# Recurrent layer: two cell products as one operation on a five-column tile, and the order of two waits turned round

## The chip, the cores and the metric

The kernel runs on one core of one Trainium2 chip. The metric is the device time of a whole execution in microseconds (us); of several runs the median is given. The profile is one execution taken by the hardware profiler. Its engines are PE (TensorE, with PEld for the load of its stationary operand), DVE (VectorE), ACT (ScalarE), POOL (GpSimd) and SP (SyncE). A `q` behind an engine (DVEq) means an instruction that the engine's sequencer carries out itself.

## What is computed

The reference is a network on a graph of 1250 nodes with 512 features: an attention layer over edges, a linear attention, a recurrent layer, a second graph layer, a second linear attention and two expert levels. The change lies in the recurrent layer alone. It takes the 1250 nodes as 1250 steps of one sequence (batch 1, hidden size 512):

```python
def step(carry, x_t):
    h_prev, c_prev = carry
    combined = jnp.concatenate((x_t, h_prev), axis=1)
    f_t = jax.nn.sigmoid(combined @ W_f + b_f)
    i_t = jax.nn.sigmoid(combined @ W_i + b_i)
    c_tilde = jnp.tanh(combined @ W_c + b_c)
    c_t = f_t * c_prev + i_t * c_tilde
    o_t = jax.nn.sigmoid(combined @ W_o + b_o)
    h_t = o_t * jnp.tanh(c_t)
    return ((h_t, c_t), h_t)
```

Each step needs h of the step before, so the steps can't overlap.

## The kernel before

The whole network is one program on one core, stage after stage with barriers between. The recurrent layer is `lstm` (line 1091). The share of x in the gates is worked out for all steps ahead of the loop into `xp`. In the loop only the 512 x 2048 product with h is left. The features stand on 128 partitions in four chunks (KC = 4). The work of a step is cut into two halves q = 0, 1 of two chunks each.

The sigmoid is taken as (1 + tanh(z/2))/2, so one tanh serves all four gates; factors of 2 go into scales. The cell variable holds twice the cell: c = 0.5 * (tanh_f + 1) * c + (tanh_i + 1) * c_tilde, and tanh is taken of 0.5 * c.

A step, engine by engine:

- PE (lines 1202 to 1232) does 128 small matmuls with h as the stationary operand. h is held in two float16 parts, a high and a low one. They are done in eight groups of 16 (`rows(par, q, k)`): three groups need only half 0 of h and start on `s_h[0]`; then PE waits for `s_h[1]` and does five more. The last group for bank 0 is the fifth of the eight and signals `s_gates[0]`; the last for bank 1 is the eighth and signals `s_gates[1]`. Twelve further matmuls into the bank `l_spare` follow, which nothing reads.
- VectorE transposes bank q into columns (`to_columns`, L1272), sums three columns for each gate (`add_up`, L1278), and after ScalarE's tanh of the gates (L1242) makes the input product `gi` (L1287), the forget product `gf` (L1288), and the open gate `go` (L1293). The cell sum is L1299. After ScalarE's tanh of the cell (L1245), `high` multiplies go by it twice (L1306 into float16, L1307 into `full`) and `low` (L1312) subtracts one from the other for the low part, which signals `s_h[q]`.
- ScalarE, after the two tanh of the gates and the two of the cell, lays the next step's input into `turn` (L1235, signal `s_input`) and copies h out (L1249).

The order on VectorE is written by hand in `step`: transpose 0, sum 0, transpose 1, gi 0, gf 0, go 0, sum 1, cell 0, gi 1, gf 1, high 0, cell 1, low 0, go 1, high 1, low 1. Engines go through their instructions in order. The order among engines comes from semaphores alone, each counted up once a step. The loop runs over two steps in each pass (`Fori(0, N, 2)`), with the sets of buffers `par` = 0 and 1.

Two VectorE operations have two waits ahead of them: the transpose of half 0 (`s_input` in `step`, then `s_gates[0]` in `to_columns`) and the first product of `high` (`s_open[q]`, then `s_tcell[q]`).

Of the kernel before, what the change touches and what calls it, by code (L numbers as in the profile page):

```python
# [11 lines left out]
ALU = mybir.AluOpType  # L12
ACT = mybir.ActivationFunctionType
# [3 lines left out]
P = 128  # L17
# [3 lines left out]
KC = C // P  # L21
# [822 lines left out]
def kernel_body(nc, d, out):  # L844

    g = Ctx(nc)
    with ExitStack() as life:
# [158 lines left out]
        linear_attention_0(g, d, x, xn)  # L1006
        g.end_phase()
        lstm(g, d, x, xn)
        g.end_phase()
        layer_1(g, d, x, xn, lo_t, dst_t, tile_node, r_table)  # L1010
# [74 lines left out]
GATES = 4  # L1085
M16 = KC * GATES
Z_BITS = 20
# [3 lines left out]
def lstm(g, d, x, h):  # L1091
# [7 lines left out]
    with ExitStack() as s0:  # L1099
        def sb(name, shape, dt=F32, scope=s0):  # L1100
            return scope.enter_context(nc.sbuf_tensor(name, shape, dt))
# [3 lines left out]
        scale = sb("l_scale", [P, 2])  # L1105
        h_scale = sb("l_h_scale", [P, 2])
        with ExitStack() as s1:
# [11 lines left out]
            with nc.Block() as block:  # L1119
                @block.gpsimd  # L1120
                def _(pool):
                    pool.partition_all_reduce(top[:, 1:2], top[:, 0:1], P, RMAX)
# [49 lines left out]
        hp = sb("l_hp", [P, 2, KC, 2 * SPREAD], F16)  # L1172
        turn = sb("l_turn", [P, 2, 2, GATES, 2 * SPREAD])
        z = sb("l_z", [P, 2, 8])
        th = sb("l_th", [P, 2, 8])
        gi = sb("l_gi", [P, KC])
        gf = sb("l_gf", [P, KC])
        go = sb("l_go", [P, KC])
        c = sb("l_c", [P, KC])
        tc = sb("l_tc", [P, KC])  # L1180
        full = sb("l_full", [P, 2, KC])
        half_h = sb("l_half_h", [P, 2])
# [4 lines left out]
        def pair(name):  # L1187
            return [s0.enter_context(g.semaphore(f"l_{name}{q}")) for q in range(2)]

        s_gates, s_turned, s_sum, s_tanh, s_terms, s_open, s_cell, s_tcell, s_full, s_h = [  # L1190
            pair(n) for n in ("gates", "turned", "sum", "tanh", "terms", "open", "cell", "tcell", "full", "h")]
        s_kept = s0.enter_context(g.semaphore("l_kept"))
        s_input = s0.enter_context(g.semaphore("l_input"))
# [36 lines left out]
        @block.scalar  # L1230
        def _(act):
            act.preload_act_table(ACT.Tanh)

            def lay_input(t, par):
                act.activation(turn[:, par, :, :, 0:34:33].rearrange("p q g v -> p q v g"),  # L1235
                               xp[:, bass.ds(t, 1), :].rearrange("p a (q v g) -> p (a q) v g", q=2, v=2),
                               ACT.Copy).then_inc(s_input, 1)

            def step(t, par):
                for q in range(2):  # L1240
                    act.wait_ge(s_sum[q], t + 1)
                    act.activation(th[:, q, :], z[:, q, :], ACT.Tanh, scale=2.0 ** -Z_BITS).then_inc(s_tanh[q], 1)  # L1242
                for q in range(2):
                    act.wait_ge(s_cell[q], t + 1)
                    act.activation(tc[:, 2 * q:2 * q + 2], c[:, 2 * q:2 * q + 2], ACT.Tanh,  # L1245
                                   scale=0.5).then_inc(s_tcell[q], 1)
                lay_input(t + 1, 1 - par)
                act.wait_ge(s_full[1], t + 1)
                act.activation(h[:, :, bass.ds(t, 1)].rearrange("p j a -> p (j a)"), full[:, par, :],  # L1249
                               ACT.Copy).then_inc(s_kept, 1)  # L1250
            act.wait_ge(s_clean, 1)
            lay_input(0, 0)
            with act.Fori(0, N, 2) as t:
                step(t, 0)
                step(t + 1, 1)

        @block.vector
        def _(dve):
            for par in range(2):
                for q in range(2):  # L1260
                    dve.memset(banks[par][q][:, :], 0.0)
            for u in range(2):
                g.link(dve, dve.tensor_copy(half_h[:, u:u + 1], h_scale[:, 0:1]))
            g.link(dve, dve.memset(c[:, :], 0.0))
            dve.memset(turn[:, :, :, :, :], 0.0).then_inc(s_clean, 1)
            g.link(dve, dve.memset(hp[:, 1, :, :], 0.0))
            dve.memset(hp[:, 0, 0:2, :], 0.0).then_inc(s_h[0], 1)
            dve.memset(hp[:, 0, 2:4, :], 0.0).then_inc(s_h[1], 1)

            def to_columns(t, par, q):  # L1270
                dve.wait_ge(s_gates[q], t + 1)
                dve.transpose(turn[:, par, q, :, 1:33],  # L1272
                              banks[par][q][:, 0:128].rearrange("p (m r) -> p m r", r=32)).then_inc(s_turned[q], 1)

            def add_up(t, par, q):
                dve.wait_ge(s_turned[q], t + 1)
                three = turn[:, par, q, :, :].rearrange("p g (v e) -> p v g e", e=SPREAD)[:, :, :, 0:3]
                dve.tensor_reduce(z[:, q, :].rearrange("p (v g) -> p v g", g=GATES), three, AX.X,  # L1278
                                  ALU.add).then_inc(s_sum[q], 1)

            def gate_of(q):
                return slice(2 * q, 2 * q + 2), th[:, q, :].rearrange("p (j q) -> p j q", q=GATES)

            def cell_terms(t, q):
                two, gate = gate_of(q)
                dve.wait_ge(s_tanh[q], t + 1)
                dve.scalar_tensor_tensor(gi[:, two], gate[:, :, 1], 1.0, gate[:, :, 3], ALU.add, ALU.mult)  # L1287
                dve.scalar_tensor_tensor(gf[:, two], gate[:, :, 0], 1.0, c[:, two], ALU.add,  # L1288
                                         ALU.mult).then_inc(s_terms[q], 1)

            def open_gate(t, q):
                two, gate = gate_of(q)
                dve.scalar_tensor_tensor(go[:, two], gate[:, :, 2], 1.0, half_h[:, :], ALU.add,  # L1293
                                         ALU.mult).then_inc(s_open[q], 1)

            def cell_sum(t, q):
                two, gate = gate_of(q)
                dve.wait_ge(s_terms[q], t + 1)
                dve.scalar_tensor_tensor(c[:, two], gf[:, two], 0.5, gi[:, two], ALU.mult,  # L1299
                                         ALU.add).then_inc(s_cell[q], 1)  # L1300

            def high(t, par, q):
                two, gate = gate_of(q)
                dve.wait_ge(s_open[q], t + 1)
                dve.wait_ge(s_tcell[q], t + 1)
                dve.tensor_tensor(hp[:, 1 - par, two, 30], go[:, two], tc[:, two], ALU.mult)  # L1306
                dve.tensor_tensor(full[:, par, two], go[:, two], tc[:, two], ALU.mult).then_inc(s_full[q], 1)  # L1307

            def low(t, par, q):
                two, gate = gate_of(q)  # L1310
                dve.wait_ge(s_full[q], t + 1)
                dve.tensor_tensor(hp[:, 1 - par, two, 31], full[:, par, two], hp[:, 1 - par, two, 30],  # L1312
                                  ALU.subtract).then_inc(s_h[q], 1)

            def step(t, par):
                dve.wait_ge(s_input, t + 1)
                to_columns(t, par, 0)
                add_up(t, par, 0)
                to_columns(t, par, 1)
                cell_terms(t, 0)  # L1320
                open_gate(t, 0)
                add_up(t, par, 1)
                cell_sum(t, 0)
                cell_terms(t, 1)
                high(t, par, 0)
                cell_sum(t, 1)
                low(t, par, 0)
                open_gate(t, 1)
                high(t, par, 1)
                low(t, par, 1)  # L1330
            with dve.Fori(0, N, 2) as t:
                step(t, 0)
                step(t + 1, 1)
            dve.wait_ge(s_h[1], N + 1)
            dve.wait_ge(s_kept, N)
            dve.scalar_tensor_tensor(x[:, :, 0:N], h[:, :, 0:N], h_scale[:, 1:2], x[:, :, 0:N], ALU.mult, ALU.add)
# [311 lines left out]
```

## Time and profile before

| | before |
|---|---|
| median of 3 runs | 8412.2 us (8410.73 to 8414.29) |
| the profiled execution | 8412.73 us, of which 8411.0 are the span from the first to the last instruction |
| mean granted TensorE clock over the span | 0.876 |
| PE busy | 5425.7 us, 65% of the span |
| DVE busy | 4210.5 us, 50% |
| ACT busy | 1532.4 us, 18% |
| POOL busy | 975.8 us, 12% |
| recurrent loop, transposes of L1272 | 2500, from 2480.9 to 6983.0 us |

The shares are means over stages with quite different limits, so they say little of the recurrent loop. It has to be read by itself: first who waits for whom, then the timeline of a single step, where each line gives the start, the duration and, in brackets, how long the engine sat idle and who ended that. The durations of VectorE and ScalarE operations overlap: the next one can start before the one ahead has reported its end, so it is the distance from start to start that an operation costs.

### The profile page before, as it was taken

What the parts mean: (1) busy time and instruction counts of PE and PEld (TensorE: products, weight loads), DVE (VectorE), ACT (ScalarE), POOL (GpSimd) and SP (SyncE); (2) the same over time, 40 slices, a digit from 0 to 9 for tenths busy, and PEclk for the clock granted to TensorE, in tenths of its full rate; (3) what the DMA queues carried; (4) which work ended last, traced back from release to release, by engine and by line L of the source; (5) the groups of instructions that cost most, each with busy time, mean ns of one, the idle gap of its engine ahead of it and who ended that gap; (6) DMA issues with size and microseconds to landing.
All of it is one profiled execution on the core that took longest, in us unless ns stands there. A gap on an engine that the chain in (4) does not pass through costs nothing. (4 is left out here: it accounts for less than half of the span.)

```text
span 8411.0 us, 418391 instructions
## 1 busy us (share of the span) xinstructions
PE 5425.7 (65%) x180989; PEld 3590.3 (43%) x180989; DVE 4210.5 (50%) x25124; ACT 1532.4 (18%) x7811; POOL 975.8 (12%) x1419
## 2 busy tenths in 40 slices
PE   1060007787787777777777777777777776675989
PEld 0020003343345555555555555555555553233435
DVE  5034446631336666666666666666666664324111
ACT  0000000011002222222222222222222221000111
POOL 1606635500000000000000000000000002510000
PEclk7585557798899999999999999999999997577889
DMA  1025553300000000000000000000000001210000
GB/s 62 16 83 161 161 106 111 108 25 25 20 20 0 0 0 0 0 0 0 0 0 0 0 0 0 0 0 0 0 0 0 0 0 42 66 43 20 0 40 13
DMA packets 117023, 236.72 MB, mean 28 GB/s; under 512 B 65357, under 2 KB 68301, under 8 KB 112986
## 3 DMA queue, kind: packets, MB, share of 16 engines
q0 software_dynamic: 56032, 162.48, 7.0%
q1 hardware_dynamic: 60922, 73.33, 2.8%
q8 instruction: 42, 0.69, 0.0%
q14 instruction: 27, 0.22, 0.0%
HBM read 221.30 MB, written 14.45 MB: 28 GB/s over the span
## 5 line engine op out<-in xcount | busy, mean ns | idle before, releaser
L1203 PE MATMUL l_bank<-l_w,l_hp 128*32 128x128 f16 x160000 | 2464.5, 219 | 1236.9 <-DVE l_hp L1312 1231.7
L1203 PEld LDWEIGHTS l_bank<-l_w,l_hp 128*32 128x32 f16 x160000 | 2246.3, 97 | 1871.2 <-DVE l_hp L1312 1865.6
L1272 DVE STREAM_TRANSPOSE l_turn<-l_bank 128x128 f32<-128x128 f32 x2500 | 791.8, 317 | 1159.7 <-PE l_bank L1203 1116.2
L1224 PE MATMUL l_spare<-l_w 128*2 128x512 f16 x15000 | 1026.0, 379 | 0.0
L1242 ACT ACTIVATE l_th<-l_z 128x8 f32<-128x8 f32 x2500 | 521.2, 208 | 2235.0 <-DVE l_z L1278 2235.0
L1245 ACT ACTIVATE l_tc<-l_c 128x2 f32<-128x2 f32 x2500 | 487.7, 195 | 548.7 <-DVE l_c L1299 548.7
L790 POOL COPY conv_idx<-dst_t 128x1 int32 x176 | 33.9, 193 | 4758.8 <-DVE conv_rows L800 4757.4
L1287 DVE SCALAR_TENSOR_TENSOR l_gi<-l_th 128x2 f32<-128x2 f32 x2500 | 381.8, 153 | 261.3 <-ACT l_th L1242 260.9
L1306 DVE TENSOR_TENSOR l_hp<-l_go,l_tc 128x2 f16<-128x2 f32 x2500 | 420.8, 168 | 179.9
L1278 DVE TENSOR_REDUCE l_z<-l_turn 128x8 f32<-128x24 f32 x2500 | 437.4, 175 | 42.6
L1312 DVE TENSOR_TENSOR l_hp<-l_full,l_hp 128x2 f16<-128x2 f32 x2500 | 422.3, 169 | 43.1
L840 PE MATMUL attend_bank<-attend_rows,attend_onehot 128*128 128x512 f32 x704 | 307.7, 582 | 165.7 <-DVE attend_onehot L813 165.0
L162 PE MATMUL forth_ends_bank<-ident,forth_ends 128*8 128x128 f32 x2 | 0.6, 395 | 601.5 <-PEq L127 601.5
L1293 DVE SCALAR_TENSOR_TENSOR l_go<-l_th,l_half_h 128x2 f32<-128x2 f32 x2500 | 383.5, 153 | 0.0
L1288 DVE SCALAR_TENSOR_TENSOR l_gf<-l_th,l_c 128x2 f32<-128x2 f32 x2500 | 383.3, 153 | 0.0
L1307 DVE TENSOR_TENSOR l_full<-l_go,l_tc 128x2 f32<-128x2 f32 x2500 | 383.1, 153 | 0.0
L1299 DVE SCALAR_TENSOR_TENSOR l_c<-l_gf,l_gi 128x2 f32<-128x2 f32 x2500 | 378.2, 151 | 0.0
L1224 PEld LDWEIGHTS l_spare<-l_w 128*2 128x2 f16 x15000 | 305.1, 84 | 152.1
L1249 ACT ACTIVATE xn<-l_full 128x4 f32 x1250 | 262.1, 210 | 409.4 <-DVE l_full L1307 409.4
L840 PE MATMUL conv_bank<-conv_rows,conv_onehot 128*128 128x257 f32 x352 | 211.5, 703 | 147.6 <-DMA conv_rows<-r_table,conv_idx 89.5
L840 PEld LDWEIGHTS attend_bank<-attend_rows,attend_onehot 128*128 128x128 f32 x704 | 160.4, 264 | 312.9 <-DVE attend_onehot L813 174.2
L632 DVE TENSOR_TENSOR q_rows<-q_rows,k_rows 128x512 f32<-128x512 f32 x176 | 124.0, 704 | 307.5 <-DMA k_rows<-k_table,score_idx 307.5
(393 smaller groups left out, 5366.6 us busy)
## 6 DMA issues: line engine op xcount, KB each, us to landing
keys<-in_src_by_tile SPq DMA_DIRECT2D x7, 1344.0 KB, 6.8
e_w<-in_e_W SPq DMA_DIRECT2D x2, 4096.0 KB
w<-in_g_W SPq DMA_DIRECT2D x2, 2048.0 KB, 10.4
l_wh<-in_l_Wh SPq DMA_DIRECT2D x1, 4096.0 KB
l_wx<-in_l_Wx SPq DMA_DIRECT2D x1, 4096.0 KB, 11.9
e_w<-in_e_W SPq DMA_DIRECT2D x2, 2048.0 KB
q_rows<-q_table,score_idx POOLq DMA_INDIRECT x176, 3.4
k_rows<-k_table,score_idx POOLq DMA_INDIRECT x176, 3.6
```

The source lines that it names most:

```text
L840: mm = pe.matmul(banks[i][:, a:b], onehot[:, i, :], rows[:, i, a:b], start=True, stop=True)
L1203: mm = pe.matmul(banks[par][q][32 * j:32 * j + 32, 0:128], hp[:, par, k, 30 - 30 * v:62 - 30 * v], w16[:, part, k, j, 256 * q + 128 * v:25 ...
L1224: pe.matmul(spare[32 * j:32 * j + 2, 0:512], w16[:, 0, k, j, 0:2], w16[:, 0, k, j, :], start=True, stop=True)
L1242: act.activation(th[:, q, :], z[:, q, :], ACT.Tanh, scale=2.0 ** -Z_BITS).then_inc(s_tanh[q], 1)
L1245: act.activation(tc[:, 2 * q:2 * q + 2], c[:, 2 * q:2 * q + 2], ACT.Tanh, scale=0.5).then_inc(s_tcell[q], 1)
L1272: dve.transpose(turn[:, par, q, :, 1:33], banks[par][q][:, 0:128].rearrange("p (m r) -> p m r", r=32)).then_inc(s_turned[q], 1)
L1278: dve.tensor_reduce(z[:, q, :].rearrange("p (v g) -> p v g", g=GATES), three, AX.X, ALU.add).then_inc(s_sum[q], 1)
L1288: dve.scalar_tensor_tensor(gf[:, two], gate[:, :, 0], 1.0, c[:, two], ALU.add, ALU.mult).then_inc(s_terms[q], 1)
L1293: dve.scalar_tensor_tensor(go[:, two], gate[:, :, 2], 1.0, half_h[:, :], ALU.add, ALU.mult).then_inc(s_open[q], 1)
L1306: dve.tensor_tensor(hp[:, 1 - par, two, 30], go[:, two], tc[:, two], ALU.mult)
L1307: dve.tensor_tensor(full[:, par, two], go[:, two], tc[:, two], ALU.mult).then_inc(s_full[q], 1)
L1312: dve.tensor_tensor(hp[:, 1 - par, two, 31], full[:, par, two], hp[:, 1 - par, two, 30], ALU.subtract).then_inc(s_h[q], 1)
```

## The change

The input product `gi` and the forget product `gf` of a half become one operation with four elements per partition. For that, the cell moves into the tile `th`: it now has five columns for each chunk, column 0 the cell, columns 1 to 4 the tanh of the gates f, i, o and c. The operation takes columns 1 and 2 (f, i), adds 1, and multiplies by columns 0 and 4 (cell, c_tilde). The results go to `terms`, whose two columns the cell sum adds into column 0 of `th`. ScalarE's tanh of the gates writes to columns 1 to 4 and the tanh of the cell reads column 0.

Of the two pairs of waits, the order in the text is turned: `s_gates[0]` now stands ahead of `s_input`, and `s_tcell[q]` ahead of `s_open[q]`. No wait is added or taken out.

```diff
--- before.py
+++ after.py
@@ -1172,11 +1172,9 @@
         hp = sb("l_hp", [P, 2, KC, 2 * SPREAD], F16)
         turn = sb("l_turn", [P, 2, 2, GATES, 2 * SPREAD])
         z = sb("l_z", [P, 2, 8])
-        th = sb("l_th", [P, 2, 8])
-        gi = sb("l_gi", [P, KC])
-        gf = sb("l_gf", [P, KC])
+        th = sb("l_th", [P, KC, GATES + 1])
+        terms = sb("l_terms", [P, KC, 2])
         go = sb("l_go", [P, KC])
-        c = sb("l_c", [P, KC])
         tc = sb("l_tc", [P, KC])
         full = sb("l_full", [P, 2, KC])
         half_h = sb("l_half_h", [P, 2])
@@ -1239,10 +1237,12 @@
             def step(t, par):
                 for q in range(2):
                     act.wait_ge(s_sum[q], t + 1)
-                    act.activation(th[:, q, :], z[:, q, :], ACT.Tanh, scale=2.0 ** -Z_BITS).then_inc(s_tanh[q], 1)
+                    act.activation(th[:, 2 * q:2 * q + 2, 1:],
+                                   z[:, q, :].rearrange("p (j m) -> p j m", m=GATES), ACT.Tanh,
+                                   scale=2.0 ** -Z_BITS).then_inc(s_tanh[q], 1)
                 for q in range(2):
                     act.wait_ge(s_cell[q], t + 1)
-                    act.activation(tc[:, 2 * q:2 * q + 2], c[:, 2 * q:2 * q + 2], ACT.Tanh,
+                    act.activation(tc[:, 2 * q:2 * q + 2], th[:, 2 * q:2 * q + 2, 0], ACT.Tanh,
                                    scale=0.5).then_inc(s_tcell[q], 1)
                 lay_input(t + 1, 1 - par)
                 act.wait_ge(s_full[1], t + 1)
@@ -1261,7 +1261,7 @@
                     dve.memset(banks[par][q][:, :], 0.0)
             for u in range(2):
                 g.link(dve, dve.tensor_copy(half_h[:, u:u + 1], h_scale[:, 0:1]))
-            g.link(dve, dve.memset(c[:, :], 0.0))
+            g.link(dve, dve.memset(th[:, :, :], 0.0))
             dve.memset(turn[:, :, :, :, :], 0.0).then_inc(s_clean, 1)
             g.link(dve, dve.memset(hp[:, 1, :, :], 0.0))
             dve.memset(hp[:, 0, 0:2, :], 0.0).then_inc(s_h[0], 1)
@@ -1269,6 +1269,8 @@
 
             def to_columns(t, par, q):
                 dve.wait_ge(s_gates[q], t + 1)
+                if q == 0:
+                    dve.wait_ge(s_input, t + 1)
                 dve.transpose(turn[:, par, q, :, 1:33],
                               banks[par][q][:, 0:128].rearrange("p (m r) -> p m r", r=32)).then_inc(s_turned[q], 1)
 
@@ -1278,42 +1280,37 @@
                 dve.tensor_reduce(z[:, q, :].rearrange("p (v g) -> p v g", g=GATES), three, AX.X,
                                   ALU.add).then_inc(s_sum[q], 1)
 
-            def gate_of(q):
-                return slice(2 * q, 2 * q + 2), th[:, q, :].rearrange("p (j q) -> p j q", q=GATES)
-
             def cell_terms(t, q):
-                two, gate = gate_of(q)
+                two = slice(2 * q, 2 * q + 2)
                 dve.wait_ge(s_tanh[q], t + 1)
-                dve.scalar_tensor_tensor(gi[:, two], gate[:, :, 1], 1.0, gate[:, :, 3], ALU.add, ALU.mult)
-                dve.scalar_tensor_tensor(gf[:, two], gate[:, :, 0], 1.0, c[:, two], ALU.add,
-                                         ALU.mult).then_inc(s_terms[q], 1)
+                dve.scalar_tensor_tensor(terms[:, two, :], th[:, two, 1:3], 1.0, th[:, two, 0:GATES + 1:GATES],
+                                         ALU.add, ALU.mult).then_inc(s_terms[q], 1)
 
             def open_gate(t, q):
-                two, gate = gate_of(q)
-                dve.scalar_tensor_tensor(go[:, two], gate[:, :, 2], 1.0, half_h[:, :], ALU.add,
+                two = slice(2 * q, 2 * q + 2)
+                dve.scalar_tensor_tensor(go[:, two], th[:, two, 3], 1.0, half_h[:, :], ALU.add,
                                          ALU.mult).then_inc(s_open[q], 1)
 
             def cell_sum(t, q):
-                two, gate = gate_of(q)
+                two = slice(2 * q, 2 * q + 2)
                 dve.wait_ge(s_terms[q], t + 1)
-                dve.scalar_tensor_tensor(c[:, two], gf[:, two], 0.5, gi[:, two], ALU.mult,
+                dve.scalar_tensor_tensor(th[:, two, 0], terms[:, two, 0], 0.5, terms[:, two, 1], ALU.mult,
                                          ALU.add).then_inc(s_cell[q], 1)
 
             def high(t, par, q):
-                two, gate = gate_of(q)
+                two = slice(2 * q, 2 * q + 2)
+                dve.wait_ge(s_tcell[q], t + 1)
                 dve.wait_ge(s_open[q], t + 1)
-                dve.wait_ge(s_tcell[q], t + 1)
                 dve.tensor_tensor(hp[:, 1 - par, two, 30], go[:, two], tc[:, two], ALU.mult)
                 dve.tensor_tensor(full[:, par, two], go[:, two], tc[:, two], ALU.mult).then_inc(s_full[q], 1)
 
             def low(t, par, q):
-                two, gate = gate_of(q)
+                two = slice(2 * q, 2 * q + 2)
                 dve.wait_ge(s_full[q], t + 1)
                 dve.tensor_tensor(hp[:, 1 - par, two, 31], full[:, par, two], hp[:, 1 - par, two, 30],
                                   ALU.subtract).then_inc(s_h[q], 1)
 
             def step(t, par):
-                dve.wait_ge(s_input, t + 1)
                 to_columns(t, par, 0)
                 add_up(t, par, 0)
                 to_columns(t, par, 1)
```

## Rows read from the trace of the kernel before

**Rows 1.** Waits in 2480:6984 us: who waited <- for whom, us in total, times, longest.
```profile
ACT l_th L1242 <- DVE l_z L1278: 2235.0, 2500, 3.5
...
PE l_bank L1203 <- DVE l_hp L1312: 1231.7, 1249, 1.1
```

**Rows 2.** Window 2481:6984: us, busy us of PE, PEld, DVE, ACT, POOL; clock, DMA.
```profile
2481.00:6984.00 4503.00, 3270.91 (x174900) 2484.35 (x174888) 2819.49 (x22492) 1313.65 (x7497) 0.00 (x0) 1.00 0.00 0
```

**Rows 3.** Line 1272 in the whole trace: count, duration ns, first and last start us.
```profile
L1272 DVE STREAM_TRANSPOSE l_turn<-l_bank x2500: 316/316/319, 2480.9 to 6983.0; 128x128 f32<-128x128 f32 x193
```

**Rows 4.** Timeline of one step: start us, us, engine, line, operation, idle before it.
```profile
4004.00 1.97 PE L1203 MATMUL l_bank<-l_w,l_hp 128*32 128x128 f16 x128 [1.04 <-DVE l_hp L1312]
...
4005.42 0.32 DVE L1272 STREAM_TRANSPOSE l_turn<-l_bank 128x128 f32<-128x128 f32 x1 [0.83 <-PE l_bank L1203]
...
4005.77 0.18 DVE L1278 TENSOR_REDUCE l_z<-l_turn 128x8 f32<-128x24 f32 x1
...
4005.98 0.21 ACT L1242 ACTIVATE l_th<-l_z 128x8 f32<-128x8 f32 x1 [1.27 <-DVE l_z L1278]
4006.02 0.32 DVE L1272 STREAM_TRANSPOSE l_turn<-l_bank 128x128 f32<-128x128 f32 x1
4006.26 0.13 DVE L1287 SCALAR_TENSOR_TENSOR l_gi<-l_th 128x2 f32<-128x2 f32 x1
...
4006.38 0.15 DVE L1293 SCALAR_TENSOR_TENSOR l_go<-l_th,l_half_h 128x2 f32<-128x2 f32 x1
4006.45 0.17 DVE L1278 TENSOR_REDUCE l_z<-l_turn 128x8 f32<-128x24 f32 x1
...
4006.65 0.21 ACT L1242 ACTIVATE l_th<-l_z 128x8 f32<-128x8 f32 x1 [0.46 <-DVE l_z L1278]
4006.77 0.19 ACT L1245 ACTIVATE l_tc<-l_c 128x2 f32<-128x2 f32 x1
4006.89 0.16 DVE L1287 SCALAR_TENSOR_TENSOR l_gi<-l_th 128x2 f32<-128x2 f32 x1 [0.21 <-ACT l_th L1242]
4006.97 0.15 DVE L1288 SCALAR_TENSOR_TENSOR l_gf<-l_th,l_c 128x2 f32<-128x2 f32 x1
4007.06 0.17 DVE L1306 TENSOR_TENSOR l_hp<-l_go,l_tc 128x2 f16<-128x2 f32 x1
...
4007.39 0.20 ACT L1245 ACTIVATE l_tc<-l_c 128x2 f32<-128x2 f32 x1 [0.44 <-DVE l_c L1299]
4007.40 0.15 DVE L1293 SCALAR_TENSOR_TENSOR l_go<-l_th,l_half_h 128x2 f32<-128x2 f32 x1
```

**Rows 5.** Timeline of the following step, beginning with PE's start.
```profile
4007.55 1.97 PE L1203 MATMUL l_bank<-l_w,l_hp 128*32 128x128 f16 x128 [0.93 <-DVE l_hp L1312]
4007.70 0.17 DVE L1306 TENSOR_TENSOR l_hp<-l_go,l_tc 128x2 f16<-128x2 f32 x1
...
4007.96 0.17 DVE L1312 TENSOR_TENSOR l_hp<-l_full,l_hp 128x2 f16<-128x2 f32 x1
...
4009.08 0.32 DVE L1272 STREAM_TRANSPOSE l_turn<-l_bank 128x128 f32<-128x128 f32 x1 [0.95 <-PE l_bank L1203]
...
4009.57 0.32 DVE L1272 STREAM_TRANSPOSE l_turn<-l_bank 128x128 f32<-128x128 f32 x1
...
4009.89 0.16 DVE L1287 SCALAR_TENSOR_TENSOR l_gi<-l_th 128x2 f32<-128x2 f32 x1
...
4010.11 0.17 DVE L1278 TENSOR_REDUCE l_z<-l_turn 128x8 f32<-128x24 f32 x1
```

**Rows 6.** Line 1271, windows 4005.35:4005.36 and 4008.90:4008.91 us, VectorE's sequencer (DVEq).
```profile
L1271 DVEq EVENT_SEMAPHORE  x1: 21/21/21, 4005.4 to 4005.4; - x1
...
L1271 DVEq EVENT_SEMAPHORE  x1: 21/21/21, 4008.9 to 4008.9; - x1
```

**Rows 7.** Line 1305, windows 4006.99:4007.00 and 4007.63:4007.64 us, VectorE's sequencer.
```profile
L1305 DVEq EVENT_SEMAPHORE  x1: 21/21/21, 4007.0 to 4007.0; - x1
...
L1305 DVEq EVENT_SEMAPHORE  x1: 21/21/21, 4007.6 to 4007.6; - x1
```

## The prediction

> **What bounds the kernel now.** I read the waits of the recurrent layer first [rows 1]. The longest are ScalarE's for the column sums (L1278) and PE's for the line that finishes h (L1312), 2235 and 1232 us: engines waiting for one another in turn, a closed loop with no engine full. TensorE's granted clock is 1.00 over the whole layer, the 2.4 GHz level [rows 2]. Next the length of a step. The transposes run 2500 times, two a step, from 2480.9 to 6983.0 us [rows 3]; the last is the second of its step, 0.6 after the first, so 1249 periods take 4501.5 us: 3.60 us a step. 1250 such steps are 4505 of the 8412.7 us, and nothing else is touched.
>
> The third view is the timeline of one step [rows 4], from PE's start at 4004.00 to the next at 4007.55: 3.55 us. The mean being 3.604, the other step of the two in a loop pass takes 3.66. This one is the pass's second step, the next its first. I name the work by half q: T is the transpose, R the reduction, th the gate tanh, tc the cell tanh. In the second step T0 starts at 5.42 (all times here are 4000 plus), R0 5.77, th0 5.98, T1 6.02, gi0 6.26, then gf0, go0 6.38, R1 6.45, th1 6.65, tc0 6.77, gi1 6.89, gf1 6.97, h0's first product 7.06, and PE again at 7.55 [rows 5]. The reader is to see which of these are held by a producer and which only by the instruction ahead. T1 comes 2.02 after PE's start, when its last matmul is out. It holds gi0: th0 was done at 6.19 but gi0 starts 0.24 behind T1. gf0, go0 and R1 follow it with some 0.07 from start to start, held by nothing but VectorE's issue. th1 follows R1 by 0.20, tc0 follows th1 by 0.12.
>
> In the first step [rows 5], PE starts at 7.55 and T1 at 9.57, again 2.02 later, but T0 starts at 9.08, 1.53 after PE instead of 1.42. It drags th0 and gi0 (9.89, 2.34 after PE, not 2.26), and R1 is at 10.11, 2.56 after PE, not 2.45. That is the whole difference between 3.66 and 3.55.
>
> The last rows say why [rows 6, 7]. An instruction with two waits stands in the program as two: an EVENT_SEMAPHORE of VectorE's sequencer and then the operation. The semaphore instruction carries line 1271 or 1305, the wait written last (s_gates, s_tcell), so the wait written first stays with the operation. At present the late signal is the one in the semaphore instruction. It passed at 5.35, and T0 started 0.07 later; at 8.90, just behind the loop's branch, and T0 started 0.18 later; at 6.99 and 7.06 for h0's product; at 7.63 and 7.70 for h1's. An operation that carries its only wait starts sooner: tanh of half 1 ends at 6.65 + 0.21 = 6.86 and gi1 starts 0.03 later, while tc0 ends at 6.77 + 0.19 = 6.96 and h0's product starts 0.10 later.
>
> **The change, part by part.** *One product fewer for each half.* In half 0, the merged operation takes gi0's place at 6.26, go0 takes gf0's place and R1 takes go0's, 6.38 instead of 6.45: 0.07 earlier. R1 has a floor: it reads T1's output, and R0 followed T0 by 0.35, so R1 can't start before 6.02 + 0.35 = 6.37. The floor is just met. In half 1 the removed gf1 is worth nothing by itself: h0's product was held by tc0 through 6.99, not by gf1. But it must be out of the way: th1 moves to 6.58, the merged operation to 6.82, and with the 0.08 from gi1 to gf1 the issue would allow 6.90.
>
> *The price of the merged operation* isn't in the trace. It has four elements with steps of 5 and 4 words, against two elements. Below: 0, an operation that costs what gi0 costs; less than gi0, with twice the elements, it has no reason to cost. Above: the TENSOR_REDUCE with 24 scattered elements takes 0.18 and the products 0.15 [rows 4], 0.02 to 0.03 more. I take 0.002, two more elements at the 1 ns each that this gap makes, as the operation is nearest to the products. The Trainium skill (Vector Engine (DVE) Microarchitecture Reference, section 5.2) speaks against a tile with five columns: an operand that hops by a few words on every element costs up to 2.5 ns a column instead of 1.05. By it, four elements would add some 6 ns, at most 12 in a step or 15 us in all, and the sum would come out at up to 8184 instead of 8171; no row here has such a step in a product of this size.
>
> *The wait for s_tcell first.* It now stays with h's product and s_open becomes the semaphore instruction. In half 0 go0 is long done, so the instruction passes at once and the product sits ready. tc0, 0.12 behind th1, starts at 6.70, ends at 6.89, and the product starts 0.03 later, 6.92. That is later than the 6.90 of issue, so tc0 sets it. Against 7.06 the two edits together give 0.14. PE follows this product by 0.49 as before: 7.41. In half 1 s_open comes from go1, which VectorE issues just ahead: 7.40 now, 7.26 then, done at 7.41, through the semaphore instruction at about 7.45, and the product 0.07 later, 7.52. So here s_open is the later of the two (tc1 would allow 7.39 + 0.20 - 0.14 + 0.03 = 7.48), and what is queued behind this wait is the two products and low h of half 1. That is 0.11 after PE's start instead of 0.15. Low h of half 1 comes 0.26 later (7.96 after 7.70 now), so it starts 0.37 after PE and ends at 0.54. PE needs it only after 48 of 128 matmuls, about 0.7 by 1.97 for all: covered, by more than now. If the cover were gone, each 0.01 there would cost 12.5 us.
>
> *The wait for s_gates first, s_input moved behind it.* T0 in the second step starts at 5.35 rather than 5.42: hidden, as T1 holds gi0's place at 6.26 (th0's result would be there at 6.15). In the first step T0 starts at 8.90 rather than 9.08, so th0's result no longer holds the products, T1 does, and the first step becomes like the second: 0.11 off. s_input comes from the copy that ScalarE issues right behind tc1 (7.39), over 1 us before T0, so the waiting instruction ahead holds nobody up. Nothing else is moved past any queue, no DMA is in this loop.
>
> *At nothing:* the tanh writing into the tile's columns 1 to 4, tc reading column 0, the sum writing there, and one memset. ScalarE took 0.21 for eight elements and 0.19 to 0.20 for two [rows 4], so shape hardly counts; each 0.01 on th1 or tc0 costs 12.5 us.
>
> **The sum.** Second step 3.55 - 0.14 = 3.41. First step 3.66 - 0.14 - 0.11 = 3.41. Mean 0.195 less, times 1250 is 244 us; the merged operation gives 2 back. From the profiled execution's 8412.7 us this leaves 8171. That execution lies 0.5 us over the median of the runs, which is nothing here.
>
> **The rivals.**
> *A, the loop's start keeps its delay.* The 0.18 behind the branch may be late arrival of the transpose itself, which no order of waits cures. For: the same pair of instructions costs 0.07 elsewhere. Against: the last operation ahead of the branch starts at 7.96 and T0 at 9.08, time enough to bring the transpose in once nothing stands blocked between. Both steps then win 0.14: 8412.7 - 175 = 8238.
> *B, the order of the waits gives nothing*, because the split into two instructions doesn't follow the text, or because both signals pay the same. Then only R1's 0.07 is left: 8412.7 - 88 = 8325. Against it stand [rows 6, 7], where the last-written wait is the separate one. The Trainium skill's rule for chained operations (VectorE: DVE Perf Modes, Rules for kernel authors), minimize the count and not the semaphores, would give this result; the 0.03 against 0.10 speaks against it.
> *C, the five-column tile is dear.* The merged operation costs 0.025 more, before R1 in full, before h0's product less 0.02 of room: 0.03, and 0.01 on the strided tanh. 0.04 a step, 50 us: about 8219.
> *D, slower.* The merged operation holds VectorE as T1 does, 0.24 to the next and not 0.08, because both inputs hop inside one tile. It stands twice in the loop: 2 x 0.16 - 0.02 = 0.30 lost against 0.195 won, 0.105 x 1250 = 131 us more: 8544. It decides from 0.11 extra on (2 x 0.11 - 0.02 = 0.20). Against: T moves 128 elements, this four, and 24 elements cost only 0.03.
>
> **Chances.** Forecast 0.66, A 0.12, C 0.10, B 0.07, D 0.03, and 0.02 for a mixture near no change. The forecast's own range comes from 0.01 of doubt in each of the terms 0.07, 0.07 and half of 0.11, about 20 us each way, so 8150 at the bottom. Upwards C and A are needed to leave out no more than 2 in 10: 8240. A change of 0.2% is about what a measurement of this kernel can tell from none. Only D lies on the slower side: faster 0.95, same 0.02, slower 0.03.
>
> **What would show it.** Both steps alike at 3.41. R1 2.38 after PE. T0 1.35 after PE in both steps. The semaphore instructions long before T0 and h0's product, and 0.03 from tc0's end to the product. The merged operation at 0.15 to 0.17. If the steps still differ by 0.11, A holds; if h0's product still comes 0.10 after tc0, B; if go0 is over 0.08 behind the merged operation, C or D. It would be wrong in another way if PE stood still after 48 matmuls, waiting for half 1.

## The result, and the profile after

The changed kernel takes 8171.7 us (median of 4 runs, 8171.0 to 8175.2) against 8411.5 us (8408.0 to 8414.3) for the kernel before: a ratio of 0.972, 95% interval 0.970 to 0.973, or 240 us less. The profiled execution took 8172.0 us, its span 8170.3.

The page of the changed kernel, its groups of instructions (busy us, mean ns of one; then the idle time ahead of them and who ended it):

```profile
L1201 PE MATMUL l_bank<-l_w,l_hp 128*32 128x128 f16 x160000 | 2464.2, 219 | 998.6 <-DVE l_hp L1310 993.4
...
L1286 DVE SCALAR_TENSOR_TENSOR l_terms<-l_th 128x4 f32<-128x4 f32 x2500 | 357.0, 143 | 256.9 <-ACT l_th L1240 256.9
L1280 DVE TENSOR_REDUCE l_z<-l_turn 128x8 f32<-128x24 f32 x2500 | 446.9, 179 | 42.6
```

PE still does its 160000 matmuls at 219 ns, but it now waits 993 us for VectorE ahead of them, where [rows 1] had 1232. VectorE has one operation fewer for each half: the merged product stands 2500 times, at a mean of 143 ns; each of the two products that it replaces took 153 ns in the mean.

A step in the timeline, from PE's start to the next (columns as in [rows 4]). It is the second of a loop pass; the last two rows belong to the first step of the next pass:

```profile
4003.35 1.97 PE L1201 MATMUL l_bank<-l_w,l_hp 128*32 128x128 f16 x128 [0.80 <-DVE l_hp L1310]
4003.47 0.17 DVE L1304 TENSOR_TENSOR l_hp<-l_go,l_tc 128x2 f16<-128x2 f32 x1
...
4003.73 0.17 DVE L1310 TENSOR_TENSOR l_hp<-l_full,l_hp 128x2 f16<-128x2 f32 x1
...
4004.71 0.32 DVE L1274 STREAM_TRANSPOSE l_turn<-l_bank 128x128 f32<-128x128 f32 x1 [0.80 <-PE l_bank L1201]
...
4005.27 0.21 ACT L1240 ACTIVATE l_th<-l_z 128x8 f32<-128x8 f32 x1 [1.24 <-DVE l_z L1280]
4005.38 0.32 DVE L1274 STREAM_TRANSPOSE l_turn<-l_bank 128x128 f32<-128x128 f32 x1
4005.62 0.12 DVE L1286 SCALAR_TENSOR_TENSOR l_terms<-l_th 128x4 f32<-128x4 f32 x1
4005.66 0.15 DVE L1291 SCALAR_TENSOR_TENSOR l_go<-l_th,l_half_h 128x2 f32<-128x2 f32 x1
4005.73 0.18 DVE L1280 TENSOR_REDUCE l_z<-l_turn 128x8 f32<-128x24 f32 x1
...
4005.94 0.21 ACT L1240 ACTIVATE l_th<-l_z 128x8 f32<-128x8 f32 x1 [0.46 <-DVE l_z L1280]
4006.05 0.19 ACT L1245 ACTIVATE l_tc<-l_th 128x2 f32<-128x2 f32 x1
4006.18 0.16 DVE L1286 SCALAR_TENSOR_TENSOR l_terms<-l_th 128x4 f32<-128x4 f32 x1 [0.21 <-ACT l_th L1240]
4006.28 0.17 DVE L1304 TENSOR_TENSOR l_hp<-l_go,l_tc 128x2 f16<-128x2 f32 x1
...
4006.54 0.17 DVE L1310 TENSOR_TENSOR l_hp<-l_full,l_hp 128x2 f16<-128x2 f32 x1
4006.61 0.20 ACT L1245 ACTIVATE l_tc<-l_th 128x2 f32<-128x2 f32 x1 [0.37 <-DVE l_th L1297]
4006.62 0.15 DVE L1291 SCALAR_TENSOR_TENSOR l_go<-l_th,l_half_h 128x2 f32<-128x2 f32 x1
...
4006.76 1.91 PE L1201 MATMUL l_bank<-l_w,l_hp 128*32 128x128 f16 x124 [0.79 <-DVE l_hp L1310]
...
4008.12 0.32 DVE L1274 STREAM_TRANSPOSE l_turn<-l_bank 128x128 f32<-128x128 f32 x1 [0.80 <-PE l_bank L1201]
```

From PE's start at 4003.35 to the next at 4006.76 the step takes 3.41 us. The reader can lay it beside [rows 4]. T0 comes 1.36 after PE (1.42 before), T1 2.03 (2.02 before). The merged product stands 0.24 behind T1, as gi0 did. The sum of half 1 (R1) follows at 2.38 after PE, not 2.45, tanh of the cell at 2.70, not 2.77, and h's product at 2.93, not 3.06. The next step's T0 stands at 4008.12, again 1.36 after PE's start at 4006.76, where [rows 5] had 1.53: the first step of a pass is no longer the slow one.

The semaphore instruction that now waits for `s_input` (line 1273, VectorE's sequencer, windows 4003.83:4003.84 and 4007.60:4007.61):

```profile
L1273 DVEq EVENT_SEMAPHORE  x1: 21/21/21, 4003.8 to 4003.8; - x1
...
L1273 DVEq EVENT_SEMAPHORE  x1: 21/21/21, 4007.6 to 4007.6; - x1
```

It passes 0.9 and 0.5 us ahead of its transpose (4004.71, 4008.12); the second of the two is the one behind the loop's branch. In [rows 6] it passed 0.07 and 0.18 ahead of it and set its start.

### The profile page after: what moved, and what is told of

The parts are those of the page before. It is cut to its first block and busy times, and to the rows that moved or that the text cites. A ratio compares the mean times of both kernels' runs of the same rounds, so it can differ in the third digit from the quotient of the medians.

```text
span 8170.3 us, 415891 instructions
## 1 busy us (share of the span) xinstructions
PE 5428.9 (66%) x180989; PEld 3593.0 (44%) x180989; DVE 4004.0 (49%) x22624; ACT 1536.1 (19%) x7811; POOL 975.0 (12%) x1419
## 5 line engine op out<-in xcount | busy, mean ns | idle before, releaser
L1245 ACT ACTIVATE l_tc<-l_th 128x2 f32<-128x2 f32 x2500 | 490.8, 196 | 463.8 <-DVE l_th L1297 463.8
L1286 DVE SCALAR_TENSOR_TENSOR l_terms<-l_th 128x4 f32<-128x4 f32 x2500 | 357.0, 143 | 256.9 <-ACT l_th L1240 256.9
L1297 DVE SCALAR_TENSOR_TENSOR l_th<-l_terms 128x2 f32<-128x2 f32 x2500 | 386.0, 154 | 0.0
L1233 ACT ACTIVATE l_turn<-l_xp 128x16 f32 (+1 forms) x1251 | 275.5, 220 | 2.6 <-DVE l_turn L1265 2.6
```

The source lines that it names most:

```text
L1245: act.activation(tc[:, 2 * q:2 * q + 2], th[:, 2 * q:2 * q + 2, 0], ACT.Tanh, scale=0.5).then_inc(s_tcell[q], 1)
L1297: dve.scalar_tensor_tensor(th[:, two, 0], terms[:, two, 0], 0.5, terms[:, two, 1], ALU.mult, ALU.add).then_inc(s_cell[q], 1)
```

## The experiments

Each stands beside runs of the kernel before from the same session. The interval is some 14 us each way, so a few us between two medians mean nothing; where a smaller difference matters, the step from the trace decides. The step is worked out from the first and last transposes of half 0, as the prediction does from [rows 3].

| kernel | median us | before us | ratio (95%) | step us |
|---|---|---|---|---|
| the change | 8171.7 | 8411.5 | 0.972 (0.970 to 0.973) | 3.41 |
| merge_only | 8327.2 | 8408.7 | 0.990 (0.989 to 0.992) | 3.54 |
| waits_only | 8304.9 | 8408.7 | 0.988 (0.986 to 0.989) | 3.52 |
| old_input_order | 8237.8 | 8408.7 | 0.980 (0.978 to 0.981) | 3.47 |
| old_cell_order | 8258.4 | 8408.7 | 0.982 (0.980 to 0.984) | 3.48 |
| five_columns_two_ops | 8305.2 | 8411.8 | 0.987 (0.986 to 0.989) | 3.52 |
| go0_behind_cell0 | 8171.2 | 8411.8 | 0.971 (0.970 to 0.973) | 3.41 |
| half1_old_order | 8172.2 | 8411.8 | 0.972 (0.970 to 0.973) | 3.41 |
| late_half1 | 8176.7 | 8411.8 | 0.972 (0.971 to 0.974) | 3.41 |
| late_half1_384b | 8276.0 | 8408.7 | 0.984 (0.983 to 0.986) | 3.50 |
| low_by_chunks | 8231.7 | 8401.9 | 0.980 (0.978 to 0.982) | 3.47 |

### One part alone: merge_only and waits_only

merge_only is the changed kernel with both pairs of waits in the old order:

```diff
-                dve.wait_ge(s_gates[q], t + 1)
                 if q == 0:
                     dve.wait_ge(s_input, t + 1)
+                dve.wait_ge(s_gates[q], t + 1)
...
-                dve.wait_ge(s_tcell[q], t + 1)
                 dve.wait_ge(s_open[q], t + 1)
+                dve.wait_ge(s_tcell[q], t + 1)
```

> The changed kernel with both pairs of waits in the old order, so the merged product and the five-column tile alone. Theory (the two edits help each other: the merged product brings the sum of half 1 forward by 0.07, the rest of its worth comes only once the late wait stays with the operation): 0.07 a step, 88 us, about 8325; both steps keep their difference of 0.11. Rival (the parts are independent and the merged product brings most of the gain, since it stands twice in the loop): two operations of 0.07, 0.14 a step, about 8237.

waits_only is the kernel before with both pairs turned round and nothing else.

> The kernel before with both pairs of waits turned round, nothing merged. Theory: h's product of half 0 may start as soon as tc0 is out (6.99 in the old timeline) but stands behind the forget product (6.97) by 0.08, so it comes at 7.05 and not at 7.06: 0.01 a step; the first step of a pass loses its extra 0.11; together 0.065 a step, 81 us, about 8331, and the two steps become equal at 3.54. This and the merged product alone then add up to 169 us of the 240 measured. Rival (independent parts): 0.07 + 0.055 a step, 156 us, about 8256.

The merged product alone is worth 82 us, the waits alone 104, together 185 before rounding; the change has both and brings 240. Some 55 us belong to neither part alone. The steps say the same without the noise of the runs: 3.604 before, 3.542 with the merged product, 3.521 with the waits, 3.413 with both, so 0.045 a step (57 us) over the sum of the two parts. The two timelines show where, at the same place of a step. In merge_only (sum of half 1, tanh of the cell of half 0, merged product of half 1, h's product):

```profile
4004.43 0.17 DVE L1280 TENSOR_REDUCE l_z<-l_turn 128x8 f32<-128x24 f32 x1
...
4004.76 0.19 ACT L1245 ACTIVATE l_tc<-l_th 128x2 f32<-128x2 f32 x1
4004.89 0.16 DVE L1286 SCALAR_TENSOR_TENSOR l_terms<-l_th 128x4 f32<-128x4 f32 x1 [0.21 <-ACT l_th L1240]
4005.05 0.17 DVE L1304 TENSOR_TENSOR l_hp<-l_go,l_tc 128x2 f16<-128x2 f32 x1
```

tc0 ends at 4004.76 + 0.19 = 4004.95, and h's product comes at 4005.05, still 0.10 later. It is held by the semaphore instruction, so the room that VectorE now has ahead of it is of no use. In waits_only (tanh of the cell, gi, gf, h's product):

```profile
4004.78 0.19 ACT L1245 ACTIVATE l_tc<-l_c 128x2 f32<-128x2 f32 x1
4004.91 0.16 DVE L1289 SCALAR_TENSOR_TENSOR l_gi<-l_th 128x2 f32<-128x2 f32 x1 [0.21 <-ACT l_th L1242]
4004.99 0.15 DVE L1290 SCALAR_TENSOR_TENSOR l_gf<-l_th,l_c 128x2 f32<-128x2 f32 x1
4005.06 0.17 DVE L1308 TENSOR_TENSOR l_hp<-l_go,l_tc 128x2 f16<-128x2 f32 x1
```

tc0 ends at 4004.97 and its signal would let the product go at 5.00; but gf of half 1 starts at 4.99 and the product stands 0.07 behind it. Here VectorE's issue sets it. Only with both parts, as in the changed kernel, does the product come 0.04 behind tc0 (6.05 + 0.19, product at 6.28). So the order alone moves this product from 0.10 to 0.09 behind tc0, and beside the merged product from 0.10 to 0.04: some 0.05 a step that neither part has alone, which is about the 0.045 left over.

The expectation for waits_only, 8331, was 26 us too high. It took 0.01 a step for half 0's product. The second step fell from 3.55 to 3.52 instead: gf, which did not have to wait for a signal, is followed by the product after 0.07 and not 0.08, and the product, which is no longer held up either, is followed by `full` after 0.07 too.

### The order of the waits, place by place: old_input_order, old_cell_order, half1_old_order

Each is the changed kernel with one of the pairs turned back; half1_old_order turns `s_open` and `s_tcell` back for half 1 alone, and this is its edit:

```diff
+                first, second = (s_tcell, s_open) if q == 0 else (s_open, s_tcell)
-                dve.wait_ge(s_tcell[q], t + 1)
-                dve.wait_ge(s_open[q], t + 1)
+                dve.wait_ge(first[q], t + 1)
+                dve.wait_ge(second[q], t + 1)
```

> The changed kernel with the waits of the transpose of half 0 back in the old order (s_gates in the separate semaphore instruction). Theory (the start of the loop pass is slow only because the transpose can't be brought in while the semaphore instruction blocks): the first step gets its delay back, T0 0.18 behind the semaphore instruction, 0.11 to 0.12 on every other step, 69 to 72 us: about 8242; the second step stays at 3.41. Rival (the order here is hidden in both steps, since T1 holds the products anyway): 8172.

It cost 66 us against the change. Two steps of its timeline:

```profile
4001.06 1.97 PE L1201 MATMUL l_bank<-l_w,l_hp 128*32 128x128 f16 x128 [0.80 <-DVE l_hp L1310]
...
4002.59 0.32 DVE L1274 STREAM_TRANSPOSE l_turn<-l_bank 128x128 f32<-128x128 f32 x1 [0.98 <-PE l_bank L1201]
...
4003.08 0.32 DVE L1274 STREAM_TRANSPOSE l_turn<-l_bank 128x128 f32<-128x128 f32 x1
...
4003.40 0.17 DVE L1286 SCALAR_TENSOR_TENSOR l_terms<-l_th 128x4 f32<-128x4 f32 x1
...
4004.58 1.97 PE L1201 MATMUL l_bank<-l_w,l_hp 128*32 128x128 f16 x128 [0.91 <-DVE l_hp L1310]
...
4006.01 0.32 DVE L1274 STREAM_TRANSPOSE l_turn<-l_bank 128x128 f32<-128x128 f32 x1 [0.88 <-PE l_bank L1201]
```

The step from 4001.06 is the first of a pass: T0 comes 1.53 after PE, the merged product waits for half 0's tanh until 3.40 instead of following T1 (3.08) by 0.24, and the step takes 3.52. The next T0 comes 1.43 after PE, later than the changed kernel's 1.36, and costs next to nothing, as T1 covers it: with a mean of 3.47 and a first step of 3.52, the second takes 3.42 where the change takes 3.41. So the order at this place is worth 0.11 in the first step and at most 0.01 in the second, as the prediction has it. What VectorE's sequencer does in the 0.18 between the semaphore instruction and T0 no view shows: the branch itself is over long before, as the instructions of the loop's end (L1331) stand at 4008.0 to 4008.3 in the kernel before and the semaphore instruction at 4008.90. Shown is only that the delay goes when the late wait stands with the transpose.

> The changed kernel with s_open ahead of s_tcell again in the text, so the late s_tcell is in the separate semaphore instruction. Theory: h's product starts 0.10 after tc0's end, not 0.03, and nothing else covers it: 0.066 in both steps, 83 us, about 8254, both steps 3.48. Rival (half 0's product has other cover and the order costs only in half 1, which PE doesn't wait for): 8172.

It cost 87 us. The place in its timeline:

```profile
4002.73 0.19 ACT L1245 ACTIVATE l_tc<-l_th 128x2 f32<-128x2 f32 x1
4002.86 0.17 DVE L1286 SCALAR_TENSOR_TENSOR l_terms<-l_th 128x4 f32<-128x4 f32 x1 [0.20 <-ACT l_th L1240]
4003.03 0.17 DVE L1304 TENSOR_TENSOR l_hp<-l_go,l_tc 128x2 f16<-128x2 f32 x1
```

tc0 ends at 4002.92 and the product starts at 3.03, 0.11 later, in every step.

> The changed kernel, where half 0 keeps s_tcell first and half 1 has s_open first again. Theory (PE has 48 of 128 matmuls to do before it needs half 1 of h, so the order in half 1 is covered): the product of half 1 comes 0.15 after PE's start instead of 0.115, time unchanged, 8172. Rival (half 1 is on the path): 0.038 a step, 48 us, about 8219.

PE's start and the product of half 1 in its timeline:

```profile
4001.28 1.97 PE L1201 MATMUL l_bank<-l_w,l_hp 128*32 128x128 f16 x128 [0.79 <-DVE l_hp L1311]
4001.43 0.17 DVE L1305 TENSOR_TENSOR l_hp<-l_go,l_tc 128x2 f16<-128x2 f32 x1
```

The product of half 1 comes 0.15 after PE's start, 0.03 to 0.04 later than in the change, and its low part starts at 0.42 instead of 0.38. The time doesn't change (8172.2 against 8171.7): of the two places where `high` waits, only that of half 0 counts.

### The price of the tile: five_columns_two_ops

The changed kernel with the merged product taken apart:

```diff
-                dve.scalar_tensor_tensor(terms[:, two, :], th[:, two, 1:3], 1.0, th[:, two, 0:GATES + 1:GATES],
-                                         ALU.add, ALU.mult).then_inc(s_terms[q], 1)
+                dve.scalar_tensor_tensor(terms[:, two, 1], th[:, two, 2], 1.0, th[:, two, 4], ALU.add, ALU.mult)
+                dve.scalar_tensor_tensor(terms[:, two, 0], th[:, two, 1], 1.0, th[:, two, 0], ALU.add,
+                                         ALU.mult).then_inc(s_terms[q], 1)
```

> The changed kernel with the merged product taken apart again into two products that read and write the same columns of the five-column tile; both pairs of waits in the new order. To be set beside waits_only (8305), which has the old separate tiles and is the same otherwise. Theory (the layout costs nothing at this size): 8305, steps of 3.52. Rival C (operands that hop by five words are dear): 0.01 to 0.04 a step more, 8318 to 8355.

8305.2 us beside 8304.9 for waits_only, which keeps the old tiles, and steps of 3.52 in both: for products of two elements the layout costs nothing that can be measured. The run says nothing of four elements; there, only the merged product's own rows speak.

### What sets the sum of half 1: go0_behind_cell0

```diff
-                open_gate(t, 0)
                 add_up(t, par, 1)
                 cell_sum(t, 0)
+                open_gate(t, 0)
```

> The changed kernel with the open gate of half 0 moved behind the cell sum of half 0, so that nothing but the merged product stands between the transpose and the sum of half 1. Theory (with the merged product the sum of half 1 has come down to its floor, 0.35 behind the transpose that it reads; one instruction less ahead of it gives nothing more): 8172, sum of half 1 still 2.38 after PE's start. Rival (VectorE's issue still sets it): 0.07 a step, 8084.

```profile
4001.81 1.97 PE L1201 MATMUL l_bank<-l_w,l_hp 128*32 128x128 f16 x128 [0.79 <-DVE l_hp L1310]
...
4003.83 0.32 DVE L1274 STREAM_TRANSPOSE l_turn<-l_bank 128x128 f32<-128x128 f32 x1
4004.07 0.12 DVE L1286 SCALAR_TENSOR_TENSOR l_terms<-l_th 128x4 f32<-128x4 f32 x1
4004.18 0.18 DVE L1280 TENSOR_REDUCE l_z<-l_turn 128x8 f32<-128x24 f32 x1
```

With the open gate out of the way, R1 stands at 4004.18, 2.37 after PE and 0.35 behind T1 (3.83): where it was. The time is the same. R1 has come down to its floor: one operation less ahead of it brought nothing.

### How much cover half 1 has: late_half1 and late_half1_384b

Both put a memset into a tile that nobody reads between the open gate of half 1 and its products; it is work added to the computation.

```diff
                 open_gate(t, 1)
+                dve.memset(idle[:, :], 0.0)
                 high(t, par, 1)
```

> The changed kernel with a memset of 128 x 256 that nobody reads between the open gate of half 1 and the products of half 1, to push half 1 of h some 0.08 to 0.1 later and so size the cover. Theory (cover of 0.05 to 0.07: PE took half 1's signal 0.02 later in the kernel before without loss): PE stands still after 48 matmuls for 0.02 to 0.05 a step, 25 to 60 us more, 8197 to 8232. Rival (no cover): the whole 0.09, 8285; rival (PE catches up on any delay): 8172.

PE's start, the memset, the two products and the low part of half 1:

```profile
4003.13 1.97 PE L1202 MATMUL l_bank<-l_w,l_hp 128*32 128x128 f16 x128 [0.80 <-DVE l_hp L1311]
4003.14 0.27 DVE L1327 MEMSET l_idle<- 128x256 f32 x1
4003.33 0.11 DVE L1305 TENSOR_TENSOR l_hp<-l_go,l_tc 128x2 f16<-128x2 f32 x1
4003.34 0.15 DVE L1306 TENSOR_TENSOR l_full<-l_go,l_tc 128x2 f32<-128x2 f32 x1
...
4003.53 0.17 DVE L1311 TENSOR_TENSOR l_hp<-l_full,l_hp 128x2 f16<-128x2 f32 x1
```

This one missed its aim. The product did move, from 0.12 to 0.20 after PE's start, but behind the memset `full` follows it by 0.01 instead of 0.07, so the low part, which waits for `full`, moved only from 0.38 to 0.40. It says no more than that 0.02 is covered; half1_old_order, with its low part at 0.42 and no time lost, says 0.04. A second version, late_half1_384, gave no time, because its edit also widened a tile of another stage. The third, with a memset of 128 x 384:

> late_half1 pushed half 1 of h by only 0.018 and so sized nothing: here the memset is 128 x 384. The low part of half 1 should start about 0.53 after PE's start instead of 0.38, its signal reach PE at 0.76. Theory (low_by_chunks, where PE took half 1 at 0.73 and lost 0.06 on every step, puts the end of the cover at 0.67): 0.09 a step lost, 112 us, about 8284. Rival (no cover beyond 0.63): 0.13 a step, 8334. Rival (PE catches up on any delay): 8172.

```profile
4002.31 2.06 PE L1202 MATMUL l_bank<-l_w,l_hp 128*32 128x128 f16 x128 [0.80 <-DVE l_hp L1311]
...
4002.64 0.10 DVE L1305 TENSOR_TENSOR l_hp<-l_go,l_tc 128x2 f16<-128x2 f32 x1
...
4002.84 0.17 DVE L1311 TENSOR_TENSOR l_hp<-l_full,l_hp 128x2 f16<-128x2 f32 x1
...
4003.75 0.32 DVE L1275 STREAM_TRANSPOSE l_turn<-l_bank 128x128 f32<-128x128 f32 x1 [0.74 <-PE l_bank L1202]
```

Low h of half 1 starts at 2.84, 0.53 after PE's start (0.38 in the change), and T0 comes 1.44 after PE's start instead of 1.36. That is 0.08 to 0.09 lost on a step, and 104 us in all: the rivals without cover (8334) and with full cover (8172) are both out. With 0.17 for the operation and some 0.05 to PE, the signal is there at 0.75; less the 0.08 to 0.09 lost, cover ends at about 0.67. The trace shows PE's wait itself: the 49th of its 128 matmuls, the first that needs half 1, starts 0.76 after PE's start here and 0.68 in the change (medians over the steps).

### A further version: low_by_chunks

```diff
-                dve.tensor_tensor(full[:, par, two], go[:, two], tc[:, two], ALU.mult).then_inc(s_full[q], 1)
...
-                dve.tensor_tensor(hp[:, 1 - par, two, 31], full[:, par, two], hp[:, 1 - par, two, 30],
-                                  ALU.subtract).then_inc(s_h[q], 1)
+                for j in (2 * q, 2 * q + 1):
+                    dve.scalar_tensor_tensor(hp[:, 1 - par, j:j + 1, 31], tc[:, j:j + 1], go[:, j:j + 1],
+                                             hp[:, 1 - par, j:j + 1, 30], ALU.mult,
+                                             ALU.subtract).then_inc(s_h[j], 1)
```

> A further version: the low part of h no longer waits for `full`. For each chunk it is one scalar_tensor_tensor, tc times go (a pointer scalar) minus the high part, straight behind the high part; `full` comes later, off the path; each chunk has its own signal to PE. In the changed kernel low h starts 0.266 behind h's product. Theory (this chain sets the period, so what is cut from it comes off in full): 0.202 from the product to the first low part (0.168 of the product and 0.034 of signal), so 0.064 a step, 80 us, about 8092, step 3.35, half 1 of h 0.61 after PE's start and covered. Rival (a pointer scalar costs VectorE 0.06 or more each time, two of them in a row): 8172 or above. Rival (PE, which now waits four times a step, loses at each wait): 8172 or above.

It is 60 us slower than the change by the medians, some 70 by the ratios. Its rows (h's product of half 0, the two low parts of half 0 in one line, PE, the low parts of half 1, T0):

```profile
4001.09 0.17 DVE L1307 TENSOR_TENSOR l_hp<-l_go,l_tc 128x2 f16<-128x2 f32 x1
...
4001.29 0.35 DVE L1312 SCALAR_TENSOR_TENSOR l_hp<-l_tc,l_go,l_hp 128x1 f16<-128x1 f32 x2
...
4001.57 2.03 PE L1202 MATMUL l_bank<-l_w,l_hp 128*32 128x128 f16 x128 [0.78 <-DVE l_hp L1312]
...
4002.02 0.35 DVE L1312 SCALAR_TENSOR_TENSOR l_hp<-l_tc,l_go,l_hp 128x1 f16<-128x1 f32 x2
...
4002.98 0.32 DVE L1277 STREAM_TRANSPOSE l_turn<-l_bank 128x128 f32<-128x128 f32 x1 [0.54 <-PE l_bank L1202]
```

The start came as expected, 0.20 behind the product. But PE starts 0.28 after it, where it starts 0.22 after the old low part (6.54 to 6.76 in the change): the operation with a pointer scalar takes 219 ns in the mean and not 169, and that eats nearly all of the 0.064. The second loss is in half 1. Its two low parts start at 0.45 after PE; the first ends at 0.67 and the second at 0.80, and T0 is at 1.41 and not 1.36. PE's 49th matmul starts at 0.73 instead of 0.68, so PE lost 0.05 waiting after its 48 matmuls. So the first rival holds, with the lost cover beside it. The second (a loss at each wait of PE) is out for the wait after 16 matmuls, which this version adds: the 17th starts 0.23 after PE's start in both kernels. No version here beats the changed kernel.

## Why the prediction was right

**What bounds the kernel.** One closed loop, in which a late start on the path through half 0's product shows up in full: old_cell_order gives back 0.07 a step for 0.07 at that one operation, while half1_old_order gives back nothing for 0.04 in half 1, and old_input_order next to nothing for 0.07 at T0 in the second step. That reading carried the rest.

**The sum.** 8171 was forecast and 8171.7 measured, both steps 3.41 as forecast. By its terms: R1 2.38 after PE, forecast 2.38, and its floor held, which go0_behind_cell0 shows by experiment. T0 at 1.36, forecast 1.35. h's product at 2.93, forecast 2.92, 0.04 behind tc0's end, forecast 0.03. PE 0.48 later, forecast 0.49. The 0.11 of the first step is gone in full, and old_input_order brings it back. Two small terms were off: R1 takes 0.18 when it has to wait for T1, and 0.17 when it stands ready (merge_only, 4004.43), so its tanh follows it by 0.21, not 0.20; and the two elements more, for which 2 us had been given, stand at no place that holds the step, as T1 sets R1 and tc0 sets the product. That the total agrees to 0.7 us is luck: by its transposes the loop gave 0.191 a step (3.604 to 3.413), 238 us and not 242, the other 2 us of the 240 lie in the spread of the runs, and the interval of the measurement is some 14 us wide each way.

**The price of the merged operation.** Taken at 2 ns with bounds 0 and 25 ns. In half 1 it takes 0.16, as gi did, and the next operation isn't held by it; in half 0 the open gate follows at 0.04. By the measured rates of the Trainium skill for operands that hop by a few words (Vector Engine (DVE) Microarchitecture Reference, section 5.2), the prediction's estimate was up to 8184. At two elements five_columns_two_ops shows nothing of such a penalty. At four, the merged product's 0.16 beside gi's 0.16 leaves no room for more than a few ns, but no run has the same product with contiguous operands.

**Half 1.** Forecast at 0.11 behind PE's start, held by `s_open` rather than `s_tcell`; measured 0.12 (4003.35 to 4003.47). Covered, as said; the cover ends near 0.67, where the prediction had "about 0.7", from a 1.97 that has the tail of the last matmul in it. The low part ends at 0.55 and its signal reaches PE at 0.60, so some 0.07 is left, less than the 0.16 between the prediction's 0.54 and 0.7, which leaves out the way to PE.

**The rivals.** A, a delay at the loop's start that no order cures, fell: the slow first step went away. Its price was right, though: old_input_order, which has the old order at this place and with it the delay, measures 8237.8 where A was put at 8238. B, the order gives nothing, fell; its price is merge_only's, 8327 against 8325. The Trainium skill's rule to minimize the count of chained operations and not their semaphores (VectorE: DVE Perf Modes, Rules for kernel authors) would have given B; here the order of the waits is worth 104 us alone, more than the operation saved, 82. C and D, a dear tile or a dear operation, fell with five_columns_two_ops and with the 0.16 of the merged product.

**Why the parts had to be summed together.** The prediction dealt with both parts at half 0's product in one line, 7.06 to 6.92, with the limit of issue (6.90) beside that of the signal (6.92). Worked out apart the parts don't add: when one of the two limits is moved alone, the other stands just behind it. Had the prediction summed part for part, 0.07 and the 0.065 expected of waits_only, it would have come out about 70 us short; by what the two parts measured alone, 55 us.

## What to carry to other kernels

In a loop that is bound by latency, look at each operation that starts late and ask for its two limits, the signal it waits for and the instruction ahead of it; a change to one gains no more than the distance to the other, so edits at one place have to be worked out together. Where an operation has two waits, find out which one the program keeps on the operation and which becomes an instruction of its own; the late signal belongs on the operation, above all behind a loop's branch. Measure which half of the work has cover before paying anything for its order.

## What the runs showed of the hardware

- After a sequencer's semaphore instruction that had to wait, the VectorE operation behind it started 0.07 later, and 0.18 later where the pair was the first behind a loop's branch [rows 6]; carrying the late wait itself, it started 0.03 to 0.04 after the producer's end.
- A VectorE operation that is held up by a signal takes some 8 ns longer than one that stands ready, and the next follows later by as much: the mean of the 2500 sums is 175 ns on the page of the kernel before and 179 ns on that of the changed one, where the half of them that belongs to half 1 came to wait for T1. In waits_only gf follows the held-up gi by 0.08 (4004.91 to 4004.99), and the product follows gf by 0.07 (5.06).
- A scalar_tensor_tensor on one element per partition with a pointer scalar took 219 ns; the one with an immediate on four elements took 143 ns in the mean (0.16 us where it had to wait for its tanh, 0.12 right behind a transpose).
